# A pipelined graph-transformer kernel: the loop over pairs of groups written out in full

## What is computed

```python
nx = ln(x); q, k, v = nx @ wq + bq, nx @ wk + bk, nx @ wv + bv     # 8 heads of 32
s = q @ k.T / sqrt(32) + where(adj > 0, 0.1 * adj * adj, -inf)
x1 = x + softmax(s) @ v @ wo + bo
x = x1 + gelu(ln(x1) @ w1 + b1) @ w2 + b2                            # 256 -> 1024 -> 256
for l in range(2):
    q, k = x @ Wq[l].T + bq[l], x @ Wk[l].T + bk[l]                  # one head of 128
    a = masked_softmax(q @ k.T / sqrt(128), adj == 0)
    x = ln(x + a @ x @ Wc[l].T) * g[l] + b[l]
```

## Time and profile before

| | |
|---|---|
| median of 3 runs | 2272.46 us (2272.21 to 2272.55) |
| profiled execution | 2277.72 us |
| its span on the core | 2275.9 us |
| PE busy | 2026.2 us (89%) |
| DVE busy | 1887.3 us (83%) |
| ACT busy | 1562.6 us (69%) |
| POOL busy | 845.8 us (37%) |
| granted TensorE clock, mean | 0.970 |

### The profile page before, as it was taken

The page is one execution under the profiler, slowest core; times in us unless marked ns, Lnnn a source line. Parts: engine busy times, 40 slices in busy tenths (PEclk is TensorE's granted clock), DMA queues, the critical chain, the costliest instruction groups (busy, mean ns, idle before and its releaser), DMA issues.

```text
span 2275.9 us, 47439 instructions
## 1 busy us (share of the span) xinstructions
PE 2026.2 (89%) x16984; PEld 1512.2 (66%) x16984; DVE 1887.3 (83%) x3589; ACT 1562.6 (69%) x2994; POOL 845.8 (37%) x632
## 2 busy tenths in 40 slices
PE   5579999999999998999999999999999999999963
PEld 3356667677677676776667677677667777767632
DVE  3677899999989898898889889898889989888543
ACT  2367777777778776777787677778777777787521
POOL 2021344333434442344444243434433344344323
PEclk8799999999999999999999999999999999999986
DMA  3221112122221021222111122221111222111000
GB/s 102 72 54 36 45 31 55 43 57 57 57 57 43 30 56 43 56 56 57 42 37 49 43 56 56 57 56 43 31 47 51 57 57 56 43 40 36 15 10 19
DMA packets 103649, 108.61 MB, mean 48 GB/s; under 512 B 9824, under 2 KB 78432, under 8 KB 103456
## 3 DMA queue, kind: packets, MB, share of 16 engines
q1 hardware_dynamic: 102912, 104.90, 17.3%
q0 software_dynamic: 544, 0.80, 0.2%
HBM read 38.55 MB, written 16.78 MB: 24 GB/s over the span
## 4 chain that ended last, share of the span: by engine, by line
PE 56%; DVE 21%; ACT 13%; issue 7%; POOL 1%; DMA 0%; SPq 0%; DVEq 0%; POOLq 0%; ACTq 0%
PE ps L245 13%; PE ps L247 13%; PE ps L246 13%; PE ps L824 5%; PE ps L1122 5%; PE ps L1048 3%; DVE hid_l L252 3%; DVE nmax L685 3%; ACT area L490 3%; DVE xh L587 2%; PE ps L1102 2%; DVE rot_l L720 2%; DVE qk L666 2%; DVE st L574 1%; ACT L490 1%
## 5 line engine op out<-in xcount | busy, mean ns | idle before, releaser
L252 POOL TENSOR_TENSOR hid_l<-area,hid_h 128x512 f16<-128x512 f32 x128 | 148.7, 1162 | 748.7 <-ACT hid_h L513 748.7
L490 ACT ACTIVATE area<-area,nbias 128x128 f32<-128x128 f32 x1024 | 313.5, 392 | 1.0 <-DVE nbias L687 0.2
L245 PE MATMUL ps<-w_h,hid_h 128*128 128x256 f16 x1024 | 279.0, 272 | 2.7 <-DVE hid_l L252 1.6
L247 PE MATMUL ps<-w_h,hid_l 128*128 128x256 f16 x1024 | 279.1, 273 | 0.0
L246 PE MATMUL ps<-w_l,hid_h 128*128 128x256 f16 x1024 | 279.1, 273 | 0.0
L510 ACT ACTIVATE area<-ps,b_col 128x512 f32<-128x512 f32 x256 | 176.1, 688 | 83.5 <-PE ps L247 82.4
L680 DVE TENSOR_TENSOR area<-ps,biasA 128x1024 f32<-128x1024 f32 x128 | 155.6, 1216 | 66.1 <-PE ps L1041 66.0
L245 PE MATMUL ps<-rot_h,w_h 128*128 128x512 f16 x512 | 195.0, 381 | 12.7 <-DVE rot_l L720 11.2
L246 PE MATMUL ps<-rot_l,w_h 128*128 128x512 f16 x512 | 194.7, 380 | 0.0
L247 PE MATMUL ps<-rot_h,w_l 128*128 128x512 f16 x512 | 194.7, 380 | 0.0
L404 POOL TENSOR_TENSOR ve<-mv,eps_cols 128x4 f32<-128x4 f32 x128 | 26.7, 209 | 418.4 <-DVE mv L579 417.5
(11 more groups left out here) (180 smaller groups left out, 6330.8 us busy)
## 6 DMA issues: line engine op xcount, KB each, us to landing
qkS<-qk SPq DMA_DIRECT2D x384, 128.0 KB, 2.3
xin<-in_x SPq DMA_DIRECT2D x32, 512.0 KB, 3.8
adj_in<-in_adj SPq DMA_DIRECT2D x64, 256.0 KB, 3.8
out<-x SPq DMA_DIRECT2D x32, 512.0 KB, 3.0
area<-in_L_gnn_w SPq DMA_DIRECT2D x2, 1024.0 KB, 11.6
area<-in_L_gnn_Wc SPq DMA_DIRECT2D x2, 256.0 KB, 11.6
area<-in_L_gnn_wq SPq DMA_DIRECT2D x1, 256.0 KB, 3.5
area<-in_L_gnn_wk SPq DMA_DIRECT2D x1, 256.0 KB, 4.3
```

Of the source, the lines that this page charges most:

```text
L245: pe.matmul(dst, lh, rh, start=start, stop=False, **kw)
L247: return pe.matmul(dst, ll, rh, start=False, stop=stop, **kw)
L252: eng.tensor_tensor(hid_l[:, c % RING, :], hidden[:, c % 2, :], hid_h[:, c % RING, :], ALU.subtract).then_inc(done, 1)
L490: last = act.activation(sc[:, b % 2, h], sc[:, b % 2, h], ACT.Exp, bias=nbias[:, b, h:h + 1], scale=1.0 / QK_SCALE)
```

## The change

`run` has no loop any more: all iterations are written out on all five engines, and each count is a constant.

```diff
@@ run @@
-            start, stop = (4 - min(aheads)) // 2, (NG - max(aheads)) // 2
-            for n in range(-max(aheads), 2 * start):
-                iteration(n // 2, n % 2)
-            with eng.Fori(start, stop) as it:
-                iteration(it, 0)
-                iteration(it, 1)
-            for n in range(2 * stop, NG - min(aheads)):
+            for n in range(-max(aheads), NG - min(aheads)):
                 iteration(n // 2, n % 2)
```

On TensorE the cases ahead of each step go through a new function. It is given signals with the number of groups that they lie behind (`behind`), and waits for the first one whose group exists; the others are left out:

```diff
+            def freed(g, *before):
+
+                pair, odd = g
+                for signal, behind, per, k in before:
+                    if not isinstance(pair, int):
+                        pe.wait_ge(signal, pair * (2 * per) + ((odd - behind) * per + k))
+                        return
+                    group = 2 * pair + odd - behind
+                    if 0 <= group < NG:
+                        pe.wait_ge(signal, group * per + k)
+                        return
+
                     if step == "Q.k0":
-                        need(pe, d_v[0], g, 1, 0)
-                        if isinstance(it, int):
-                            need(pe, d_o, g, B, -4)
+                        freed(g, (d_v[0], 1, 1, 1))
...
                     elif step == "C0.q":
-                        need(pe, d_cT[0], g, 1, 1)
-                        if isinstance(it, int):
-                            need(pe, d_xT, g, 1, 4)
-                            need(pe, d_cy[1], g, 1, -1)
+                        freed(g, (d_cT[0], 0, 1, 1))
...
                     elif step == "Q.k1":
-                        need(pe, d_qk[1], g, 1, 1)
-                        if isinstance(it, int):
-                            need(pe, a_gelu, g, FC, -9)
+                        freed(g, (d_qk[1], 0, 1, 1))
```

More of the change, by code:

```diff
@@ L893, in iteration @@
-                        if isinstance(it, int):
-                            need(pe, d_xT, g, 1, 4)
-                            need(pe, d_cy[1], g, 1, -1)
+                        freed(g, (d_cS[0], 0, 1, 1))
+                        freed(g, (a_ck[0], 0, 1, 1))
                     elif step == "Q.q1":
-                        need(pe, a_gelu, g, FC, -9)
-                        if isinstance(it, int):
-                            need(pe, d_v[1], g, 1, 0)
+                        freed(g, (a_gelu, 2, 8, 7), (d_v[1], 1, 1, 1))
@@ L925, in iteration @@
                     elif step == "C1.xT":
[L926 to L930, removed]
+                        freed(g, (a_cPT[0], -1, 1, 1), (d_cy[1], 1, 1, 1), (d_cy[0],
+                              0, 1, 1))
+                        freed(g, (a_cW[0], -1, 1, 1), (d_cy[1], 1, 1, 1), (d_cy[0],
+                              0, 1, 1))
@@ L947, in iteration @@
+                        freed(g, (d_cT[1], 1, 1, 1), (a_cW[0], 0, 1, 1))
                     elif step == "A.wo":
-                        need(pe, d_oT, g, 1, 1)
+                        freed(g, (d_oT, 0, 1, 1))
                     elif step == "C1.q":
-                        need(pe, d_cy[0], g, 1, 2)
-                        if isinstance(it, int):
-                            need(pe, d_cT[1], g, 1, 1)
-                            need(pe, d_xT, g, 1, 5)
+                        freed(g, (d_cy[0], -1, 1, 1), (d_cT[1], 0, 1, 1))
@@ L972, in iteration @@
-                        need(pe, a_ck[1], g, 1, 1)
-                        if isinstance(it, int):
-                            need(pe, d_cy[0], g, 1, 2)
-                            need(pe, d_xT, g, 1, 5)
+                        freed(g, (d_cS[1], 0, 1, 1))
+                        freed(g, (a_ck[1], 0, 1, 1))
                     elif step == "M.mT":
-                        need(pe, d_x2, g, 1, 0)
+                        freed(g, (d_x2, 1, 1, 1))
                     elif step == "A.S1":
-                        need(pe, d_S, g, B, 1)
+                        freed(g, (d_S, 0, 4, 1))
@@ L999, in iteration @@
+                        freed(g, (a_cPT[1], 0, 1, 1))
                     elif step == "A.PT0":
[L1000 removed]
+                        freed(g, (d_S, 0, 4, 2))
                     elif step == "M.up1":
[L1002 to L1004 removed]
+                        freed(g, (a_gelu, 0, 8, 1))
                     elif step == "N.xT":
[L1006 removed]
@@ L1007, in iteration @@
-                        if isinstance(it, int):
-                            need(pe, d_cy[0], g, 1, -3)
-                            need(pe, d_xT, g, 1, 0)
+                        freed(g, (d_cy[1], 5, 1, 1), (d_cy[0], 4, 1, 1), (d_xT, 1,
+                              1, 1))
                     elif step == "M.down0":
-                        need(pe, d_mT, g, 1, 1)
+                        freed(g, (d_mT, 0, 1, 1))
                     elif step == "M.up2":
-                        need(pe, a_gelu, g, FC, 2)
@@ L1014, in iteration @@
-                        if isinstance(it, int):
-                            need(pe, d_v[1], g, 1, 2)
+                        freed(g, (a_gelu, 0, 8, 2))
                     elif step == "C0.xT":
-                        need(pe, d_xT, g, 1, 4)
-                        if isinstance(it, int):
-                            need(pe, d_cy[1], g, 1, -1)
-                            need(pe, d_cy[0], g, 1, 0)
+                        freed(g, (d_xT, -3, 1, 1), (d_cy[1], 2, 1, 1), (d_cy[0], 1,
+                              1, 1))
```

117 lines of the change are left out of this document (28 added, 89 removed).

## The result

Written out, the kernel takes 2261.26 us (median of 10 runs, 2256.45 to 2270.84) against 2272.8 us (10 runs, 2270.64 to 2278.53) for the kernel before on the same chip: ratio 0.995, 95% interval 0.9933 to 0.9967. It is faster by 0.5%. The gain is 11.5 us where the prediction had 6.7. Its profiled execution took 2262.16 us, 0.9 over its median; that of the kernel before lay 4.9 over its own, so the two profiles are 4 us further apart than the medians.

A forecast was written before the change was run, and what follows sets the result against it. TensorE, busy 89%, was taken as nearly the bound, with some path in instructions that wait for nothing shown. Jumps 4.7 plus register work 2.0, other terms 0, made 6.7 us: 2272.46 to 2265.8 us, range 2257 to 2280.

The forecast's parts named there:

- The sum from two forms in one trace: Group time: 64.93 us written out ahead of the loop against 65.55 in it; the gain summed to 6.7 us.
- The jump, 0.47 us each: TensorE's jump back, in ten groups: each taken jump removed saves 0.47 us of group time, 4.7 us in all.
- half of the jump's cost is hidden behind that: Group behind a jump: VectorE, late by its own 2.47 us subtraction ahead of qk, hides half the jump's cost.
- The register work, 0.18 us: Register arithmetic ahead of waits in the loop, 830 ns a group on VectorE: 0.18 us reaches the end, 2.0 in all.
- Fewer waits, 0: TensorE outside the loop: dropped second and third waits bring nothing, at most 0.8 us.
- Code fetches, 0: Queue 14 fetches the other engines' written-out code throughout; this costs nothing, at worst 3.4 us for a late fetch.
- The clock: Low-clock stretches behind the qk wait, 1.6 us each: five taken as before, between none and eight.
- fewer stretches: Rival: all five low-clock stretches go too, 2257.8 us; within the 0.50 for as many stretches or fewer.
- The rate of 0.31 per whole wait: Low-clock stretches followed 5 of 16 whole qk waits; for 26 groups that would be 8.
- In step, slower: Rival: equal groups fall to the low clock together; eight stretches more give 2278.6 us, all 26 give 2299; chance 0.17.
- The whole stall back: Rival: all 19.4 us of TensorE's issue waits lie on the path, 21.4 us go, 2251.1 us; chance 0.02.
- It doesn't do what it says: Rival: queue 14's fetches or SyncE's issues get in the way and take some gain, 2268 to 2273 us; chance 0.02.

The follow-up runs named there:

- the loop with the new waits: Kernel before, loop kept on all engines, only TensorE's chain of waits outside the loop replaced by the change's shorter one: 2254.94 us, ratio 0.9911.
- written out with the old waits: Changed kernel, all engines written out, but TensorE keeps its old chain with the second and third waits: 2270.62 us, ratio 0.9967 to before.
- two buffers: Changed kernel with two x3 buffers in turn, so GpSimd waits for the store of two groups ago: 2258.86 us, ratio 0.9929 to before.
- qk first: Changed kernel with VectorE's qk (Q.q1) moved ahead of the subtraction M.lo6: 2227.33 us, ratio 0.9796 to before.

## Why the prediction was right, and where its steps were wrong

*The sum from two forms in one trace: right in size.* A written-out group was put at 64.93 us; the 26 measure 1687.5 / 26 = 64.90. Reading the new form off the old trace worked. That this form was also the faster one hung on where the loop's code happened to lie: against the loop with the new waits, whose code lies elsewhere (2254.94 us), writing it out gains nothing. In that the sign was luck.

*The jump, 0.47 us each: wrong cause.* I took it for the stall less what DVE's lateness hides. It is a stall that is more than covered (a jump group without a fetch in the store lasts 64.2 to 64.8 us, less than a plain one) plus 0.9 us (65.4 against 64.5) where the fetch falls on the store's last word, 0.67 of them by GpSimd's later start. With another position of the code, the same ten jumps cost less than nothing: 64.49 against 64.8 to 64.9 written out. The step that failed is "half of the jump's cost is hidden behind that", which named DVE's own 2.47 us as the reason for the wait.

*The register work, 0.18 us: size short, place wrong.* It is 65.1 against 64.8, 0.3 us, and it isn't DVE's alone, on whose 830 ns of register operations I had hung it. That it is register work at all is argued: the loop form differs by little else in a plain group.

*Fewer waits, 0: right for the wait, wrong for the edit.* No array wait changed. But dropped instructions move all code behind them, and with the loop kept 26 groups took 16.4 us less, 9 of them by the jump groups and 8 by five low-clock stretches fewer, whose cause isn't shown. I had bounded the cost of what each instruction takes, not of where it puts the others.

*Code fetches, 0: wrong.* Their price is not a sequencer that runs dry, of which no trace here shows a case outside the jumps, but a late DMA: 0.2 to 0.7 us in five of the eight groups of 65.0 to 65.5, 1.9 us in the worst one. The Trainium skill, "Runtime: NRT & Kernel Launch", section "Instruction fetch mechanics", calls the crossing of a block mostly hidden. For the fetching engine the trace agrees (no wait of PE for "issue" in 26 groups); for a store whose end others wait for it doesn't (up to 5.0 us instead of 3.1). The row that could have told me stood in the earlier trace rows: jump groups kept a 1.1 us wait for qk, which a stall of 1.8 alone should have taken from 2.2 to 0.4. It is 0.4 where the store lands in 2.90 us.

*The clock: forecast as five, measured as none.* 5 x 1.6 = 8.0 us of the 15.2 in the profiles. The rival "fewer stretches" said 2257.8 us; the two medians are 2261.26 and 2257.81, the last an agreement that is partly chance. I had too little weight on it. The rate of 0.31 per whole wait didn't hold: 26 waits of 2.0 to 2.3 us gave 0 twice here, 5 written out with the old waits, 9 with TensorE alone written out. What decides between these isn't settled. The size of a stretch held nearly: 66.2 against 64.5 us, 1.7, with two buffers.

*In step, slower:* not in this kernel. TensorE alone written out came nearest with nine stretches in 26 and still was 0.2% faster than before. *The whole stall back* (2251.1 us): no, though the loop with new waits reached 2254.94 by another way. *It doesn't do what it says:* in one sense it held, without the loss that I had tied to it. Writing out the loop gave nothing over the new waits with the loop.

## What to carry to other kernels

Before pricing a loop's jump, follow the wait behind it one releaser further than the engine that the profile names: here an elementwise step was held by GpSimd, GpSimd by a store, and the store by a fetch of code. An edit that only adds or drops instructions moves every later fetch, so a difference of half a per cent between two forms may be the place of the code; shift the code alone before the form gets the credit. And follow a resource that two engines share past the first victim: with the store out of the way GpSimd held another instruction of VectorE instead. The remedy that lasts is to take the exposed step out from behind the shared resource: one swap on VectorE gave 31 us, over six times what the jumps had seemed to cost.

## What the runs showed of the hardware that was not expected

- A packet of code of 16 KB can hold up the last of a store's 16 final words. GpSimd started 2.90 us after the issue in jump groups without it and 3.1 in plain ones; 3.53 to 3.66 with the packet and the last word both 3.0 us behind the issue; 4.5 to 5.0 where the packet came 1.0 or 1.9 us behind it (four cases in three kernels), 3.8 to 4.6 where it came 0.6 to 0.8 us behind it (five cases); a packet of 8 KB on queue 14 at 1.9 us: 3.8. Many packets at 2.5 to 3.1 us held up nothing (nine of eleven in the loop with the new waits). What tells the two kinds apart isn't in the records.
- A subtraction of VectorE takes 0.68 us with GpSimd idle and up to 2.55 beside a GpSimd step of 2.36 us, ending 0.55 us after it in every group. Small instructions with one input are held too: `nbias` took 1.7 us instead of 0.2 beside such a step, 26 times out of 26 (two `x3`), and `cmax` 2.26 instead of 0.17.
- 2 us of idle PE in a group of 65 us can be followed by 3.4 us at 1.2 GHz, at 1.6 us each; with qk first and all written out, with one `x3` or two, no wait for an input was above 1.15 us and no group had one. With waits of 1.1 and 0.5 us close together (two `x3`) five had.
